# An attention and feed-forward kernel on one core: half of the score bounds computed by VectorE instead of GpSimd, weight loads spread over earlier stages, one activation table set for exponential and logarithm

## Chip, core and metric

One Trainium2 chip, one of its cores. The metric is the device time of one execution in microseconds (us). The profile shows one execution; its engines are named PE (TensorE matmul), PEld (TensorE weight load), DVE (VectorE), ACT (ScalarE), POOL (GpSimd) and SP (SyncE, which issues DMAs).

## What is computed

4096 tokens of 256 channels pass through two layers. The first layer adds a state-space recurrence and a mixture of 64 experts (6 per token); the second adds an attention and a gated feed-forward net. The change touches the second layer's attention. There, for each token, the 16 heads are the *positions* that attend to each other's channels: with Q, K and V reshaped to 16 x 64,

```
Q, K, V = ((x @ W + b).reshape(b, s, H, C) for each of the three)      # H, C = 16, 64; Q also times 1/8
scores = jnp.einsum('bshq,bshk->bshqk', Q, K)                          # an outer product of channels, per token and head
scores = jnp.where(triu(ones((C, C)), 1), -inf, scores)                # key channel k only up to query channel q
w = softmax(scores, axis=-1)
attn = jnp.einsum('bshqk,bshk->bshq', w, V).reshape(b, s, H * C)
y = attn @ Wo + bo + down(silu(gate(x)) * up(x))
```

So there is no matrix product in the attention itself: per token and head it is 64 x 64 / 2 products, exponentials and sums.

## The kernel before

The program is a sequence of stages with a barrier between them: routing; the recurrence; `routed_experts` (32 turns of 8 blocks); `combine` (adds the six expert outputs of each token, normalises, and stores x and its transpose); and `attention_and_ffn`, which takes three quarters of the time. In `combine` SP loads the expert outputs in a ring of five (L1065) and, after the first five, all weights of the last stage in one go (L1073 to L1080): bo, the three projections (1 MB each), three biases spread over the partitions, Wo, and three integer weights that VectorE turns into floats (L985 on).

`attention_and_ffn` works through 32 tiles of 128 tokens. A tile has 24 chunks: 0 to 7 are the triangle of the first half of the query channels, 8 to 15 the rectangle of second half queries on first half keys (2048 elements per partition each), 16 to 23 the triangle of the second half. The triangles' chunks have 2048, 256, 1536, 768, 1024, 1280, 512, 1792 and 2048, 1792, 1536, 1280, 1024, 256, 512, 768 elements. Every chunk goes through five steps on four engines:

- **product** (VectorE, `products`, L1215 and L1216, output `at_s`): query by key, the keys held in a PSUM bank `at_kp`;
- **subtraction** (GpSimd, L1280, in place on `at_s`): minus `at_m`, the greatest score that this query can have;
- **exponential** (ScalarE, L1365, in place);
- **value product** (VectorE, `times_v`, L1215 and L1216, output `at_pv`): times V, held in the PSUM bank `at_vp`;
- **row sums** (TensorE, L1525) of the exponentials into `at_den`, and of the value products into `at_num`.

The order on each engine is written out by hand in that engine's `tile(t, u)`, a loop over the chunk number c; VectorE makes the product of chunk c (one ahead in chunks 4 to 8) and then the value product of chunk c - 3. Beside the chunks each engine has small tasks at fixed c. TensorE projects the next tile's K at c = 4 and 8, its first query half at c = 17 and its first value half at c = 19, all into one shared PSUM bank `at_work`, so each projection waits until the one before has been read. ScalarE reads the query projection out in `keep_q` (c = 19 for the next tile's first half, c = 0 for the second half). At c = 18 it does the `silu` of the feed-forward net, which needs another table set than the exponential.

The bound `at_m` is needed by a tile's subtractions: max(q, 0) times the running maximum of the keys (`at_k_top`) minus max(-q, 0) times the running minimum (`at_k_low`). VectorE scans the keys (`scan`, c = 8 to 13). ScalarE writes max(q, 0) into `at_m` and max(-q, 0) into `at_fall` (L1318, L1320), and GpSimd does the rest in `maxima`, three operations of 512 elements (L1260, L1262, L1265), for the second half of this tile after chunks 3, 4, 5 and for the first half of the next tile after chunks 21, 22, 23. The first two read the scans `turned`, that is channels descending, with a step of 64 floats from one element to the next:

```
turned = lambda x: view(x[:], [[-1, RANGE], [C, H]], h * RANGE + RANGE - 1)
MAXIMA_HERE, MAXIMA_NEXT = {3: 0, 4: 1, 5: 2}, {21: 0, 22: 1, 23: 2}
```

Of the kernel before, what the change touches and what calls it, by code (L numbers as in the profile page):

```python
# [6 lines left out]
ALU = mybir.AluOpType  # L7
# [640 lines left out]
def routed_experts(nc, k, io, scratch):  # L648
# [3 lines left out]
    with ExitStack() as ctx:  # L652
# [36 lines left out]
        with nc.Block(no_gpsimd_drain=True) as block:  # L689
# [189 lines left out]
            def _(sp):  # L879
# [27 lines left out]

                for i in range(TURNS):
                    turn_in(i)


def combine(nc, k, io, scratch):
    with ExitStack() as ctx:
# [14 lines left out]
        x2_done, x2_out, bo_in, w_in, dequant = (a.sem(s) for s in ("x2", "x2_out", "bo_in", "w_in", "dequant"))  # L928
        y_in, xT_out = [a.sem(f"y_in{j}") for j in range(RING)], [a.sem(f"xT_out{j}") for j in range(TURN_RING)]
        dve_step, pool_step = a.sem("dve"), a.sem("pool")  # L930
        members = lambda g: slice(g * GROUP, (g + 1) * GROUP)
        with nc.Block(no_gpsimd_drain=True) as block:
# [11 lines left out]
            def _(dve):  # L944
# [10 lines left out]
                def weights(step):  # L955

                    if step == 0:
                        dve.wait_ge(w_in, 160)
# [15 lines left out]
                    elif step == 4:  # L974
                        c(v.tensor_copy(parts[96:128, :], rest[96:128, :]))
                    else:
                        dequantise(step - 5)
# [82 lines left out]
            def _(sp):  # L1060
# [13 lines left out]
                for i, name in enumerate(("WqT", "WkT", "WvT")):  # L1074
                    sp.dma_start(k.wqkv[i][:], io[name].rearrange("(c p) n -> p c n", p=P)).then_inc(w_in, 16)
                for i, name in enumerate(("bq", "bk", "bv")):
                    sp.dma_start(rest[:, i * HC:(i + 1) * HC], io[name].partition_broadcast(P)).then_inc(w_in, 16)
                sp.dma_start(k.wo[:], io["Wo"].rearrange("(c p) n -> p c n", p=P)).then_inc(w_in, 16)
                for i, (name, c) in enumerate((("wgT", DC), ("wuT", DC), ("wdT", HT))):
                    sp.dma_start(stage[i][:].rearrange("p (c n) -> p c n", c=c),  # L1080
                                 io[name].rearrange("(c p) n -> p c n", p=P)).then_inc(w_in, 16)
# [10 lines left out]
                sp.wait_ge(x2_out, 16 * NT // GROUP)  # L1092
                for j in range(TURN_RING):
# [22 lines left out]
FIRST, BODY = 2, 10  # L1116


def attention_and_ffn(nc, k, io, scratch):
    with ExitStack() as ctx:  # L1120
# [27 lines left out]
        work_done, k_out, q_out, v_out, up_out, scanned, max_step = (  # L1148
            a.sem(s) for s in ("work_done", "k_out", "q_out", "v_out", "up_out", "scanned", "max_step"))
# [68 lines left out]
        with nc.Block() as block:  # L1218
# [32 lines left out]
            def _(pool):  # L1251
                def maxima(t, h, step):

                    n = t * 2 + h
                    turned = lambda x: view(x[:], [[-1, RANGE], [C, H]], h * RANGE + RANGE - 1)
                    rows = lambda x, at=0: view(x[:], [[H, RANGE], [1, H]], at)
                    if step == 0:
                        pool.wait_ge(scanned, t * 4 + 4)
                        pool.wait_ge(q_out, n + 1)
# [3 lines left out]
                    else:  # L1263
                        pool.wait_ge(max_step, n * 3 + 2)
# [457 lines left out]
```

## Time and profile before

| | us |
|---|---|
| median of 3 runs (lowest to highest) | 3786.36 (3785.81 to 3789.21) |
| the profiled execution's own time | 3785.92 |
| its span, first to last instruction | 3784.2 |
| `combine`, about | 785 to 910 of the span |
| `attention_and_ffn`, about | 910 to 3784 of the span |
| one tile of it | 88.6 |
| busy in the whole span: PE, DVE, POOL, ACT | 3491.1, 3234.1, 3306.9, 1968.9 |
| mean granted clock of TensorE | 0.972 |

In the views, "idle before" is the time in which an engine did nothing before an instruction, with what ended it; a row of the timeline has the start, the length, the engine, the line, the operation, out<-in, and the count of merged instructions. Lengths of neighbours on one engine overlap by some hundredths of a us, so what an instruction takes of its engine is read from start to start. The granted clock is a share of TensorE's upper level.

### The profile page before, as it was taken

The page shows a single profiled execution, that of the slowest core. Times are in us where ns is not written, and L with a number is a line of the kernel's source. Part 1 is how long each engine was busy: PE and PEld are TensorE (multiplying, and loading weights), DVE is VectorE, ACT ScalarE, POOL GpSimd, SP SyncE. Part 2 cuts the span into 40 slices and gives each one's busy share as a digit, 9 for nine tenths or more (in the row PEclk, how much of TensorE's full clock was granted, in tenths as well). Part 3 has the DMA queues.
Part 4 walks back from the last instruction along what each step waited for, and adds up shares of the span by engine and source line. Part 5 has one row for each costly group of instructions (what it writes and reads, how often), then busy time and mean ns, then how long its engine had stood idle before and what let it go on. Part 6 is the DMA issues. An engine that isn't in the chain of part 4 may idle for free.

```text
span 3784.2 us, 72605 instructions
## 1 busy us (share of the span) xinstructions
PE 3491.1 (92%) x25868; PEld 3068.3 (81%) x26061; DVE 3234.1 (85%) x3516; ACT 1968.9 (52%) x2519; POOL 3306.9 (87%) x1507
## 2 busy tenths in 40 slices
PE   3684999967999999999999999999999999999999
PEld 2343988855888888888888888888888888888888
DVE  8422677757999999999999999999999999999998
ACT  1100434444555555665665566555555665665565
POOL 1677555523999999999999999999999999999998
PEclk7797999988999999999999999999999999999999
DMA  9523566685000000000000000000000000000000
GB/s 377 179 102 111 183 191 199 198 302 198 4 5 5 5 5 5 7 5 5 8 5 6 5 5 5 6 5 5 5 5 6 7 5 6 7 5 5 5 5 5
DMA packets 110619, 209.17 MB, mean 55 GB/s; under 512 B 16608, under 2 KB 77280, under 8 KB 110304
## 3 DMA queue, kind: packets, MB, share of 16 engines
q1 hardware_dynamic: 84192, 140.90, 11.4%
q0 software_dynamic: 21504, 59.93, 4.3%
q8 instruction: 191, 3.13, 0.3%
q10 hardware_dynamic: 4608, 4.20, 0.3%
q14 instruction: 124, 1.02, 0.1%
HBM read 183.34 MB, written 107.74 MB: 77 GB/s over the span
## 4 chain that ended last, share of the span: by engine, by line
POOL 43%; issue 31%; PE 1%; DVE 0%; ACT 0%; POOLq 0%; DMA 0%; ACTq 0%; DVEq 0%
POOL at_s L1280 38%; POOL at_m L1265 2%; POOL at_fall L1262 2%; POOL at_m L1260 2%; POOLq L1279 0%; DVE at_pv L1216 0%; PE at_work L1502 0%; PE at_num L1525 0%; ACT at_s L1365 0%; POOL at_hid L1270 0%; DVE at_s L1216 0%; DMA at_xT<-xT 0%; PE at_num L1502 0%; PE at_den L1525 0%; PE at_misc L1551 0%
## 5 line engine op out<-in xcount | busy, mean ns | idle before, releaser
L1280 POOL TENSOR_TENSOR at_s<-at_s,at_m 128x2048 f32<-128x2048 f32 (+7 forms) x768 | 2507.1, 3306 | 5.4 <-POOL at_m L1265 4.5
L1365 ACT ACTIVATE at_s<-at_s 128x2048 f32<-128x2048 f32 (+7 forms) x768 | 1081.7, 1417 | 952.6 <-POOL at_s L1280 952.2
L1525 PE MATMUL at_num<-k_ident,at_pv 128*128 128x128 f32 (+2 forms) x9216 | 1135.6, 273 | 65.5 <-DVE at_pv L1215 54.6
L1525 PE MATMUL at_den<-k_ident,at_s 128*128 128x128 f32 (+2 forms) x9216 | 1137.5, 273 | 19.7 <-ACT at_s L1365 17.2
L1525 PEld LDWEIGHTS at_num<-k_ident,at_pv 128*128 128x128 f32 (+2 forms) x9216 | 1025.3, 139 | 150.7 <-DVE at_pv L1215 84.3
L1525 PEld LDWEIGHTS at_den<-k_ident,at_s 128*128 128x128 f32 (+2 forms) x9216 | 1028.5, 139 | 57.8 <-ACT at_s L1365 21.2
L1216 DVE TENSOR_TENSOR at_pv<-at_s,at_vp 128x2048 f32<-128x2048 f32 (+7 forms) x512 | 690.6, 1349 | 122.1 <-PE at_num L1525 66.5
L1216 DVE TENSOR_TENSOR at_s<-at_q,at_kp 128x2048 f32<-128x2048 f32 (+7 forms) x512 | 689.9, 1348 | 27.4 <-PE at_den L1525 23.8
L1215 DVE TENSOR_TENSOR at_pv<-at_s,at_vp 128x2048 f32<-128x2048 f32 x256 | 583.9, 2281 | 0.0
L1215 DVE TENSOR_TENSOR at_s<-at_q,at_kp 128x2048 f32<-128x2048 f32 x256 | 581.4, 2271 | 0.0
L706 POOL DMA_INDIRECT picked<-moe_yo,moe_row x256 | 245.8, 960 | 171.0 <-ACT moe_yo L761 82.9
L1502 PE MATMUL at_work<-k_region,at_xT 128*128 128x512 f32 x776 | 367.0, 595 | 7.4 <-DMA at_xT<-xT 7.4
L142 POOL DMA_INDIRECT slot_x<-e_xn,e_slot x192 | 190.6, 993 | 136.9 <-DMA slot_x<-k_region 75.7
L728 PE MATMUL moe_gu<-moe_xT,c_w 128*128 128x128 f32 x2048 | 278.3, 279 | 5.6 <-DVE moe_xT L850 5.6
L728 PEld LDWEIGHTS moe_gu<-moe_xT,c_w 128*128 128x128 f32 x2048 | 250.3, 193 | 17.2 <-DVE moe_xT L850 13.1
L1502 PEld LDWEIGHTS at_work<-k_region,at_xT 128*128 128x128 f32 x776 | 132.9, 191 | 101.5 <-issue 93.6
L767 ACT ACTIVATE moe_gate<-moe_gu 128x128 f32<-128x128 f32 x256 | 71.0, 277 | 269.5 <-PE moe_gu L728 269.5
L1512 PE MATMUL at_work<-at_xT,k_region 128*128 128x128 f32 x1536 | 187.2, 275 | 0.0
L1512 PEld LDWEIGHTS at_work<-at_xT,k_region 128*128 128x128 f32 x1536 | 179.1, 192 | 0.0
L844 DVE TENSOR_TENSOR moe_hid<-moe_gate,moe_gu 128x128 f32<-128x128 f32 x256 | 73.4, 287 | 104.7 <-ACT moe_gate L767 101.3
L735 PE MATMUL moe_yp<-c_w,moe_hid 128*128 128x256 f32 x512 | 153.5, 382 | 0.3 <-DVE moe_hid L844 0.3
L850 DVE COPY moe_xT<-moe_tr 128x256 f32<-128x256 f32 x256 | 107.1, 418 | 46.5 <-PE moe_tr L719 45.1
(249 smaller groups left out, 3171.2 us busy)
## 6 DMA issues: line engine op xcount, KB each, us to landing
c_w<-experts SPq DMA_DIRECT2D x256, 384.0 KB
slot_x<-k_region SPq DMA_DIRECT2D x16, 2144.0 KB, 25.1
moe_x<-slot_x SPq DMA_DIRECT2D x256, 134.0 KB, 2.2
cmb_y<-picked SPq DMA_DIRECT2D x32, 768.0 KB, 7.8
at_xT<-xT SPq DMA_DIRECT2D x33, 128.0 KB, 2.0
e_x<-u SPq DMA_DIRECT2D x4, 1024.0 KB, 9.5
picked<-moe_yo,moe_row POOLq DMA_INDIRECT x256
xT<-cmb_xT ACTq DMA_DIRECT2D x32, 128.0 KB, 6.0
```

What stands on the lines that cost most here:

```text
L142: nc.gpsimd.indirect_dma_start(scratch["slot_x"], bass.IndirectOffsetOnAxis(ap=k.slot[:, n, j:j + 1], axis=0), k.xn[:, n, :], None).then_i ...
L706: pool.indirect_dma_start(scratch["picked"], bass.IndirectOffsetOnAxis(ap=row[i % 2][:, j:j + 1], axis=0), yo[j][:], None).then_inc(y_out[ ...
L728: ins = nc.tensor.matmul(gu[j % 2][:, s, :], w[j][:, (2 * s + c) * P:(2 * s + c + 1) * P], xT[j][:, c, :], start=(c == 0), stop=(c == DC - 1))
L735: nc.tensor.matmul(yp[j % 2][:], hid[j][:], w[j][:, 2 * D:3 * D], start=True, stop=True).then_inc(y_done, 1)
L850: nc.vector.tensor_copy(xT[j][:], tr[j % 2][:]).then_inc(xT_ready, 1)
L1215: return nc.vector.tensor_tensor(by_row(out), by_row(other), keys, ALU.mult)
L1216: return nc.vector.tensor_tensor(out, other, keys, ALU.mult)
L1280: nc.gpsimd.tensor_tensor(part(s_slot, c), part(s_slot, c), by_query(m[unit_of(c)][:], c), ALU.subtract).then_inc(sub_done, 1)
L1365: nc.scalar.activation(part(s_slot, c), part(s_slot, c), ACT.Exp, scale=C ** -0.5).then_inc(exp_done, 1)
L1502: nc.tensor.matmul(into[:], xT[u][:, c, :], wqkv[which][:, c, cols], start=(c == 0), stop=False)
L1512: ins = nc.tensor.matmul(work[:, (2 * s + h) * P:(2 * s + h + 1) * P], w[:, c, tile * P:(tile + 1) * P], xT[u][:, c, :], start=(c == 0), s ...
L1525: ins = nc.tensor.matmul(dst[0:wide, b * P:(b + 1) * P], buf[:, at:at + wide], k.ident[:], start=(c in (0, NTRI) and x == 0 and b == 0), s ...
```

## The change

**Maxima.** For the first query half, ScalarE now copies the projection only (`keep_q` returns after the copy), and VectorE makes the bound in three operations that read the projection's bank directly: `at_m` = `at_k_top` x q, the bank = `at_k_low` x q (in place), `at_m` = the greater of the two. The first two stand at VectorE's c = 20, the third at c = 21, of the tile before. GpSimd keeps the second half's maxima. TensorE's next projection into that bank (its c = 19) now waits for the third operation.

**Table sets.** A table set with both exponential and logarithm is loaded before the stage and after each `silu`.

**Loads.** The three projections are loaded in turns 10, 18 and 26 of `routed_experts`, biases, integer weights and Wo between the loads of `combine`'s ring. (One small tensor, gamma, moves to another place in a shared region.)

```diff
 # routed_experts, SyncE
+                def load_projection(which):
+                    tiles = (which + 1) * HC * DC // D
+                    sp.wait_ge(own_added, tiles)
+                    sp.dma_start(k.wqkv[which][:], io[("WqT", "WkT", "WvT")[which]].rearrange("(c p) n -> p c n", p=P)
+                                 ).then_inc(k.wqkv_in, 16)
+                PROJECTION = {10: 0, 18: 1, 26: 2}
                 for i in range(TURNS):
                     turn_in(i)
+                    if i in PROJECTION:
+                        load_projection(PROJECTION[i])
...
 # combine, SyncE
+                BIAS, STAGE, WO = {5: 0, 6: 1, 7: 2}, {9: 0, 11: 1, 13: 2}, 16
                 for n in range(RING, NT):
                     load(n)
+                    if n in BIAS:
+                        load_bias(BIAS[n])
+                    if n in STAGE:
+                        load_stage(STAGE[n])
+                    if n == WO:
+                        sp.dma_start(k.wo[:], io["Wo"].rearrange("(c p) n -> p c n", p=P)).then_inc(w_in, 16)
...
 # attention_and_ffn, GpSimd
-                MAXIMA_HERE, MAXIMA_NEXT = {3: 0, 4: 1, 5: 2}, {21: 0, 22: 1, 23: 2}
+                MAXIMA_HERE = {3: 0, 4: 1, 5: 2}
...
-                        if c in (0, NTRI):
-                            pool.wait_ge(max_step, t * 6 + (3 + 3 * unit_of(c)))
+                        if c == 0:
+                            pool.wait_ge(max0_step, t * 3 + 3)
+                        if c == NTRI:
+                            pool.wait_ge(max_step, t * 3 + 3)
...
-                        if c in MAXIMA_NEXT:
-                            maxima(t + 1, 0, MAXIMA_NEXT[c])
...
 # ScalarE, keep_q
+                    if h == 0:
+                        nc.scalar.copy(q[h][:, FRONT:QL], source[:]).then_inc(q_out, 1)
+                        return
...
 # ScalarE, end of silu
+                    nc.scalar.preload_act_table_set(EXP_AND_LN)
...
 # VectorE
+                def maxima(t, step, source=work):
+                    turned = lambda x: view(x[:], [[-1, RANGE], [C, H]], RANGE - 1)
+                    rows = lambda x, at=0: view(x[:], [[H, RANGE], [1, H]], at)
+                    if step == 0:
+                        dve.wait_ge(q_out, t * 2 + 1)
+                        dve.wait_ge(scanned, t * 4 + 4)
+                        wait(dve, sub_done, (t - 1) * NCH + NTRI)
+                        v.tensor_tensor(rows(m[0], FRONT), turned(k_top), rows(source), ALU.mult).then_inc(max0_step, 1)
+                    elif step == 1:
+                        dve.wait_ge(max0_step, t * 3 + 1)
+                        v.tensor_tensor(rows(source), turned(k_low), rows(source), ALU.mult).then_inc(max0_step, 1)
+                    else:
+                        dve.wait_ge(max0_step, t * 3 + 2)
+                        v.tensor_tensor(m[0][:, FRONT:QL], source[:], m[0][:, FRONT:QL], ALU.max).then_inc(max0_step, 1)
...
+                MAXIMA_NEXT = {20: (0, 1), 21: (2,)}
...
+                        for step in MAXIMA_NEXT.get(c, ()):
+                            maxima(t + 1, step)
...
 # TensorE, c = 19
                         pe.wait_ge(q_out, t * 2 + 3)
+                        pe.wait_ge(max0_step, t * 3 + 6)
                         project(t + 1, 1 - u, 2, 0)
```

VectorE in the second triangle of a tile, before, with what each waits for: the product of chunk 20, the value product of chunk 17, the first step of a division, the product of 21 and the value product of 18 (`at_exp` is the exponential's semaphore, `at_q_out` that of `keep_q`).

```order
L1216 TENSOR_TENSOR at_s<-at_q,at_kp 128x1024 [waits at_pv,at_den_done]
L1216 TENSOR_TENSOR at_pv<-at_s,at_vp 128x1792 [waits at_num_done,at_exp]
L1440 TENSOR_TENSOR at_den<-at_den,at_inv 128x512 [waits at_inv_ready]
L1216 TENSOR_TENSOR at_s<-at_q,at_kp 128x256 [waits at_pv,at_den_done]
L1216 TENSOR_TENSOR at_pv<-at_s,at_vp 128x1536 [waits at_num_done,at_exp]
L1443 SCALAR_TENSOR_TENSOR at_log_den<-at_den,at_inv 128x512 [waits at_newton]
```

The same place in the changed kernel:

```order
L1240 TENSOR_TENSOR at_s<-at_q,at_kp 128x1024 [waits at_pv,at_den_done]
L1240 TENSOR_TENSOR at_pv<-at_s,at_vp 128x1792 [waits at_num_done,at_exp]
L1471 TENSOR_TENSOR at_m<-at_k_top,at_work 128x512 [waits at_sub,at_scanned,at_q_out]
L1474 TENSOR_TENSOR at_work<-at_k_low,at_work 128x512 [waits at_max0_step]
L1484 TENSOR_TENSOR at_den<-at_den,at_inv 128x512 [waits at_inv_ready]
L1240 TENSOR_TENSOR at_s<-at_q,at_kp 128x256 [waits at_pv,at_den_done]
L1240 TENSOR_TENSOR at_pv<-at_s,at_vp 128x1536 [waits at_num_done,at_exp]
L1477 TENSOR_TENSOR at_m<-at_work,at_m 128x512 [waits at_max0_step]
L1487 SCALAR_TENSOR_TENSOR at_log_den<-at_den,at_inv 128x512 [waits at_newton]
```

Two operations came in behind the value product of chunk 17, the first with a wait for ScalarE's copy of the query, and one behind that of chunk 18.

ScalarE around its c = 18 and 19 in the changed kernel: the exponential of chunk 18 (1536 elements), `silu` between two table loads, the exponential of chunk 19 (1280), the copy of the next tile's query.

```order
L1391 ACTIVATE at_s<-at_s 128x1536
L1379 ACT_TABLE_LOAD
L1379 ACTIVATE at_hid<-at_gu_sb 128x768
L1380 ACT_TABLE_LOAD
L1391 ACTIVATE at_s<-at_s 128x1280
L1339 COPY at_q<-at_work 128x512
L1391 ACTIVATE at_s<-at_s 128x1024
```

Before, the same stood there with two more activations behind the copy (into `at_m` and `at_fall`); the four other table loads of a tile, two in front of each logarithm and exponential of the denominators, are gone elsewhere.

## Rows read from the trace of the kernel before

**Rows 1.** Page, part 1: busy us (share of the span) x instructions, whole span.

```profile
PE 3491.1 (92%) x25868; PEld 3068.3 (81%) x26061; DVE 3234.1 (85%) x3516; ACT 1968.9 (52%) x2519; POOL 3306.9 (87%) x1507
```

**Rows 2.** Busy us, sum and mean of twelve tiles' stretches; last numbers: mean per engine.

```profile
sum 1063.80, PE 1037.83 PEld 935.48 DVE 1011.63 ACT 636.13 POOL 1060.56; mean PE 86.49 PEld 77.96 DVE 84.30 ACT 53.01 POOL 88.38
```

**Rows 3.** Timeline of VectorE from chunk 20 to the next tile's start.

```profile
1625.28 2.02 DVE L1216 TENSOR_TENSOR at_pv<-at_s,at_vp 128x1792 f32<-128x1792 f32 x1
1627.21 0.69 DVE L1440 TENSOR_TENSOR at_den<-at_den,at_inv 128x512 f32<-128x512 f32 x1
1627.82 0.41 DVE L1216 TENSOR_TENSOR at_s<-at_q,at_kp 128x256 f32<-128x256 f32 x1
...
1629.81 0.69 DVE L1443 SCALAR_TENSOR_TENSOR at_log_den<-at_den,at_inv 128x512 f32<-128x512 f32 x1
...
1634.99 2.29 DVE L1216 TENSOR_TENSOR at_s<-at_q,at_kp 128x2048 f32<-128x2048 f32 x1
...
1642.64 1.22 DVE L1216 TENSOR_TENSOR at_s<-at_q,at_kp 128x1024 f32<-128x1024 f32 x1 [0.71 <-PE at_den L1525]
1647.18 2.29 DVE L1216 TENSOR_TENSOR at_pv<-at_s,at_vp 128x2048 f32<-128x2048 f32 x1 [3.31 <-PE at_num L1525]
```

**Rows 4.** Timeline of ScalarE around chunks 18 and 19 and the next tile's start.

```profile
1623.11 1.49 ACT L1365 ACTIVATE at_s<-at_s 128x1536 f32<-128x1536 f32 x1 [0.73 <-POOL at_s L1280]
1624.62 1.28 ACT L1354 ACT_TABLE_LOAD   x1
1625.91 0.84 ACT L1354 ACTIVATE at_hid<-at_gu_sb 128x768 f32<-128x768 f32 x1
1626.77 1.28 ACT L1365 ACT_TABLE_LOAD   x1
1628.07 1.28 ACT L1365 ACTIVATE at_s<-at_s 128x1280 f32<-128x1280 f32 x1
1629.24 0.57 ACT L1316 COPY at_q<-at_work 128x512 f32<-128x512 f32 x1
...
1646.48 0.61 ACT L1340 COPY at_vp<-at_v 128x512 f32<-128x512 f32 x1
```

**Rows 5.** Timeline of GpSimd, end of one tile and of the next.

```profile
1549.73 4.55 POOL L1280 TENSOR_TENSOR at_s<-at_s,at_m 128x2048 f32<-128x2048 f32 x1 [0.16 <-POOL at_m L1265]
...
1630.87 1.56 POOL L1260 TENSOR_TENSOR at_m<-at_k_top,at_m 128x512 f32<-128x512 f32 x1
...
1633.62 1.53 POOL L1262 TENSOR_TENSOR at_fall<-at_k_low,at_fall 128x512 f32<-128x512 f32 x1
...
1636.89 1.28 POOL L1265 TENSOR_TENSOR at_m<-at_m,at_fall 128x512 f32<-128x512 f32 x1
1638.34 4.56 POOL L1280 TENSOR_TENSOR at_s<-at_s,at_m 128x2048 f32<-128x2048 f32 x1 [0.17 <-POOL at_m L1265]
```

**Rows 6.** Timeline of VectorE: one instruction that waits for another; first idle time of `combine`.

```profile
793.71 0.42 DVE L1003 TENSOR_TENSOR e_x<-e_x,cmb_acc 128x256 f32<-128x256 f32 x1 [1.57 <-PE cmb_acc L1025]
794.17 0.43 DVE L1005 BATCH_NORM_STATS2 cmb_stats<-e_x 128x6 f32<-128x256 f32 x1
...
821.88 0.48 DVE L983 SCALAR_TENSOR_TENSOR e_x<-cmb_y,e_choice_w,e_x 128x256 f32<-128x256 f32 x1 [20.39 <-DMA cmb_y<-picked]
```

**Rows 7.** Groups of VectorE instructions, 780 to 785 us: busy us, mean ns.

```profile
L873 DVE TENSOR_REDUCE moe_weight_sum<-e_choice_w 128x32 f32<-128x192 f32 x1 | 0.5, 482 | 0.0
L876 DVE TENSOR_TENSOR e_choice_w<-e_choice_w,moe_weight_sum 128x192 f32<-128x192 f32 x1 | 0.4, 358 | 0.0
```

**Rows 8.** Timeline of TensorE at its c = 19: the next tile's value projection.

```profile
1633.54 1.88 PE L1502 MATMUL at_work<-k_region,at_xT 128*128 128x512 f32 x4
```

**Rows 9.** Busy us per stretch (length, engines, PEclk, DMA share, GB/s): experts' end, `combine`.

```profile
700.00:770.00 70.00, 69.05 (x521) 62.72 (x520) 49.28 (x173) 28.02 (x87) 41.40 (x43) 1.00 0.70 215
790.00:822.00 32.00, 12.34 (x51) 10.32 (x51) 5.78 (x18) 9.31 (x31) 1.27 (x2) 0.71 1.03 382
822.00:907.00 85.00, 72.89 (x334) 59.95 (x334) 71.88 (x167) 47.91 (x147) 13.82 (x14) 0.94 0.91 327
```

More of the change, by code:

```diff
@@ L976, in weights @@
                     else:
+                        dve.wait_ge(stage_in, 48)
                         dequantise(step - 5)
@@ L1073, in _, with load_bias, load_stage @@
                 sp.dma_start(bo[:], io["bo"].partition_broadcast(P)).then_inc(bo_in, 16)
[L1074 to L1079, printed above, removed]
+                def load_bias(i):
+                    sp.dma_start(rest[:, i * HC:(i + 1) * HC], io[("bq", "bk", "bv")[i]].partition_broadcast(P)
+                                 ).then_inc(bias_in, 16)
+                def load_stage(i):
+                    name, c = (("wgT", DC), ("wuT", DC), ("wdT", HT))[i]
                     sp.dma_start(stage[i][:].rearrange("p (c n) -> p c n", c=c),
-                                 io[name].rearrange("(c p) n -> p c n", p=P)).then_inc(w_in, 16)
+                                 io[name].rearrange("(c p) n -> p c n", p=P)).then_inc(stage_in, 16)
+                BIAS, STAGE, WO = {5: 0, 6: 1, 7: 2}, {9: 0, 11: 1, 13: 2}, 16
                 for n in range(RING, NT):
                     load(n)
+                    if n in BIAS:
[4 more added lines that the diff above has]
+                        sp.dma_start(k.wo[:], io["Wo"].rearrange("(c p) n -> p c n", p=P)).then_inc(w_in, 16)
                     if n % GROUP == 0 and n >= 3 * GROUP:
@@ L1092, in _ @@
                 sp.wait_ge(x2_out, 16 * NT // GROUP)
+                sp.wait_ge(w_in, 16)
+                sp.wait_ge(k.wqkv_in, 48)
                 for j in range(TURN_RING):
@@ L1116 @@
 FIRST, BODY = 2, 10
+EXP_AND_LN = "natural_log_exp_and_others"
 def attention_and_ffn(nc, k, io, scratch):
@@ L1147, in attention_and_ffn @@
         xT_in = [a.sem(f"xT_in{u}") for u in range(2)]
-        work_done, k_out, q_out, v_out, up_out, scanned, max_step = (
-            a.sem(s) for s in ("work_done", "k_out", "q_out", "v_out", "up_out", "scanned", "max_step"))
+        work_done, k_out, q_out, v_out, up_out, scanned, max_step, max0_step = (
+            a.sem(s) for s in ("work_done", "k_out", "q_out", "v_out", "up_out", "scanned", "max_step",
+                              "max0_step"))
         kp_ready, vp_ready, mult_done, sub_done, exp_done, pv_done = (
@@ L1251, in _, with maxima @@
             def _(pool):
-                def maxima(t, h, step):
-                    n = t * 2 + h
+                def maxima(t, step):
+                    h = 1
                     turned = lambda x: view(x[:], [[-1, RANGE], [C, H]], h * RANGE + RANGE - 1)
@@ L1282, in tile @@
                         if c in MAXIMA_HERE:
-                            maxima(t, 1, MAXIMA_HERE[c])
-                        if c in MAXIMA_NEXT:
-                            maxima(t + 1, 0, MAXIMA_NEXT[c])
+                            maxima(t, MAXIMA_HERE[c])
                         if c == GATED:
@@ L1293, in _ @@
                     nc.gpsimd.memset(t[:, FULL:FULL + TAIL], 0.0).then_inc(zeroed, 1)
-                for step in range(3):
-                    maxima(0, 0, step)
                 pool.wait_ge(padded, 4)
@@ L1318, in keep_q @@
                     nc.scalar.activation(m[h][:, FRONT:QL], source[:], ACT.Relu)
-                    wait(act, max_step, n * 3)
+                    wait(act, max_step, t * 3)
                     nc.scalar.activation(fall[:], source[:], ACT.Relu, scale=-1.0).then_inc(q_out, 1)
@@ L1391, in tile @@
                             show_k(t + 1, 1 - u, 0)
+                nc.scalar.preload_act_table_set(EXP_AND_LN)
                 keep_k(0, 0, 0)
@@ L1427, in scan @@
                         dve.wait_ge(work_done, use)
-                        wait(dve, max_step, t * 6)
+                        wait(dve, max_step, t * 3)
+                        wait(dve, max0_step, t * 3)
                         v.tensor_tensor_scan(k_top[:, cols], flat(keep_max), source[:], 0.0, ALU.add, ALU.max
@@ L1486, in _ @@
                         scan(0, half, step, half + 1, source=(work, first_k)[half])
+                for step in range(3):
+                    maxima(0, step, source=first_q)
                 dve.wait_ge(padded, 4)
@@ L1614, in _ @@
                 pe.wait_ge(q_out, 1)
+                pe.wait_ge(max0_step, 3)
                 pe.wait_ge(v_out, 1)
@@ L1643, in carve @@
         return parts
-    k.xnT, k.bT, k.cT, k.sgT, k.suT, k.sdT, k.gamma, k.beta, k.zeros, k.bu = carve(first)
+    k.xnT, k.bT, k.cT, k.sgT, k.suT, k.sdT, k.beta, k.zeros, k.bu, k.gamma = carve(first)
     k.xs, k.xnT = k.xnT, k.xnT.rearrange("p n (c t) -> p n c t", c=DC)
```

10 lines of the change are left out of this document (6 added, 4 removed).

## The prediction

> **What bounds the kernel now.** I read the page's busy shares first: TensorE, GpSimd and VectorE are at 85% or more and ScalarE is at half [rows 1], so the shares alone name no bound. The stretches tile by tile, second, do: in a tile of 88.65 us (1063.80 / 12) GpSimd works 88.4, TensorE 86.5, VectorE 84.3 [rows 2]. GpSimd has no slack. VectorE's 4.3 us of idle time are not spread: the timeline shows 0.71 and 3.31 us just ahead of and at the tile's first value product [rows 3]. The label there is TensorE, but what ended the wait is ScalarE's copy into `at_vp`, over at 1646.48 + 0.61 = 1647.09, and VectorE starts at 1647.18 [rows 3, 4]. That copy stands behind the exponential of chunk 0, hence behind GpSimd's subtraction of chunk 0, hence behind VectorE's product of chunk 0. So this idle time follows VectorE's own product; it is not a reserve that can be spent anywhere. A tile's length is 1638.34 - 1549.73 = 88.61 us, from one subtraction of chunk 0 to the next [rows 5].
>
> **The maxima, what is removed.** GpSimd loses three operations a tile, all between the subtractions of chunk 21 and the next chunk 0: 1.56, 1.53 and 1.28 us, 4.4 in all [rows 5]. ScalarE loses two activations behind its copy. If GpSimd alone decided, a tile would fall to 84.2.
>
> **What is added, and where it waits.** The first new VectorE operation needs ScalarE's copy of the query. Before, that copy ends at 1629.24 + 0.57 = 1629.81 [rows 4], and VectorE reaches the place, behind the value product of chunk 17, at 1627.21 [rows 3]. So VectorE would stand 2.60 us in front of it. The copy can't come earlier: it stands behind the exponential of chunk 19, this behind table load, `silu`, table load, and these behind the exponential of chunk 18, which follows GpSimd's subtraction of chunk 18 (ScalarE waited 0.73 us for it) [rows 4]. Behind the waiting instruction on VectorE are all products of chunks 21, 22, 23 and of the next tile's chunk 0, so GpSimd, which gained 4.4 us just there, gets nothing to work on.
>
> This closes a loop, and its length is the new tile. Step by step: (a) from a subtraction of chunk 0 to the copy's end, 1629.81 - 1549.73 = 80.08 us: in it GpSimd runs without a pause up to chunk 18 and ScalarE from there, and nothing of it is removed. (b) From the copy to VectorE's start 0.09, as after `at_vp` above. (c) First maximum. A 512-element operation on a PSUM bank lasts 0.69 and takes 0.61 of the engine [rows 3]. Its successor waits for it, which costs the full length and 0.04 (794.17 against 793.71 + 0.42 [rows 6]): 0.73. For its reading with a step between elements I add 0.33: the strided reduction of 192 elements takes 482 ns, a plain operation of 192 takes 358 [rows 7], 0.65 ns an element, times 512. So 1.06. (d) Second maximum: 0.61 + 0.33 = 0.94. (e) What VectorE does today from the division to the end of the next tile's product of chunk 0: 1634.99 + 2.29 - 1627.21 = 10.07 [rows 3]; in its midst the third maximum, 0.61. (f) To the subtraction's start 0.17, as today [rows 5]. The sum is 80.08 + 0.09 + 1.06 + 0.94 + 10.07 + 0.61 + 0.17 = 93.02 us, 4.41 more than 88.61. There are 31 passages from one tile to the next: 31 x 4.41 = 136.7 us.
>
> The one price in it that the trace doesn't show directly is the strided reading. Its lower end is nothing (0.66 us a tile, 20 us in all, less); the upper is the value taken, which is the nearest row. The Trainium skill, in VectorE: DVE Perf Modes, Mode 1x (REGULAR), says of the baseline mode that "weird strides" work and a result comes each cycle; by that the penalty would be nothing and the sum 20 us lower. The strided row speaks against it, but it is another operation, and no row here shows the very one.
>
> **TensorE's new wait.** Its c = 19 projection starts at 1633.54 [rows 8]. In the changed order the third maximum ends at 1629.81 + 0.09 + 1.06 + 0.94 + 2.60 + 0.69 = 1635.19 (2.60 for the division, product 21 and value product 18, 1629.81 - 1627.21 [rows 3]): TensorE is held 1.65 us, with row sums queued behind. It has 88.6 - 86.5 = 2.1 us idle a tile and gets 4.4 more, so I take 0 for it; if it weren't made up, 31 x 1.65 = 51 us.
>
> **Table sets.** Four loads of 1.28 us [rows 4] a tile leave ScalarE. It is busy 53 of 88.6 us [rows 2], and none of the four lies in the loop above (the two around `silu` stay). Cost and gain 0.
>
> **Loads.** Today VectorE waits 20.39 us in `combine` for the sixth expert output [rows 6], behind the weights, while DMA is full (1.03); afterwards DMA is still 0.91 busy and VectorE 71.9 of 85 us [rows 9]. So only what leaves the stage is won: three projections, 3.1 MB, at 382 to 327 GB/s [rows 9] 8 to 9.6 us; I take 9. The ends are 0 (if VectorE's and TensorE's own work fills the time) and the whole 20.4. In the experts' stage DMA has 0.30 of 70 us free [rows 9], 21 us, and a projection needs about 3 us; TensorE is the bound there with 69.05 of 70. SP issues each one behind a turn's loads, and the states it waits for are added two turns earlier. I take 1 us for all three, between 0 and 10. The first tile's maxima change one for the other: 0. The last tile's delay the drain, where TensorE is last: 1, between 0 and 4.4.
>
> **Sum.** 3785.92 (the profiled execution's own time) + 136.7 - 9 + 1 + 1 = 3915.6. The median of the runs is 0.4 above that execution: **3916 us**, 3.4% slower. With the ends of the terms this case spans 3881 (no stride penalty, 20 us from the loads) to 3938.
>
> **Rivals.** *A, faster:* VectorE doesn't wait, because its idle 4.0 us move from the tile's start to the copy and the moved work lands in slack. Then VectorE is the bound: 84.3 + 2.6 = 86.9 us a tile, just above TensorE's 86.5: 31 x -1.7 = -53, and with the loads 3786 - 53 - 9 + 2 = 3726. It decides by one thing, whether the copy ends before VectorE is through with chunk 17's value product; for it speaks that GpSimd is the busiest engine, against it the 2.60 us above, and that the idle time at the tile's start comes behind the product of chunk 0 in any case. The Trainium skill (Perfetto Trace Analysis, Identifying the Most-Contended Engine) would have the engine with the highest occupancy, here GpSimd, relieved first, and by it this rival would be the forecast. The trace bears the occupancy out but shows a loop that leaves GpSimd's relieved place aside. *B, no change:* the added wait and the idle time at the tile's start cancel, a tile stays at 88.6 and only the loads count: 3786 - 9 + 2 = 3779. It would need a shorter chain from chunk 0's product to `at_vp`, of which the change removes nothing. *C, slower still:* TensorE can't make up its 1.65 us: 3916 + 51 = 3967. For it, 86.5 busy of 88.6; against it, the longer tile. That the table loads or the loads stay where they were is excluded by the order of the instructions.
>
> **How the numbers follow.** The forecast 0.80, A 0.10, B 0.05, C 0.05. A change of 0.2%, 7.6 us, is about what a measurement of this kernel can tell from none; B lies on that edge, so I give 0.03 of it to no change and 0.02 to faster. Faster 0.12, same 0.03, slower 0.85. The range takes in the forecast's own 3881 to 3938 and a part of what lies beyond it on both sides (TensorE not making up all): 3870 to 3945.
>
> **What would show it.** Right: a tile of about 93 us; on VectorE a wait of some 2.6 us in front of the first maximum, ended by ScalarE; GpSimd busy about 84 us a tile and idle ahead of chunks 21 to 0, waiting for VectorE's products; the first two maxima about 1.0 us long, the third 0.7; two table loads a tile; `combine` shorter by some 9 us with no idle time of 20. Wrong: a tile under 88.6 us, or the first maximum starting with no wait. That the maxima last 0.7 us throughout would take 20 us off and leave the rest standing.

## The result, and the profile after

| us | before | after |
|---|---|---|
| median (lowest to highest) | 3787.36 (3785.81 to 3789.21), 4 runs | 3911.37 (3909.72 to 3912.42), 4 runs |
| profiled span | 3784.2 | 3910.6 |
| first load of the attention issued | 910.60 | 898.20 |
| from there to the end | 2873.6 | 3012.4 |
| one tile | 88.61 | 93.04 |

After / before is 1.0327 (95%: 1.0315 to 1.034): slower by 124 us, within the range given, 5 us below the forecast. The attention is 138.8 us longer and begins 12.4 us earlier.

The page of the changed kernel, busy us in the whole span, answers to [rows 1]. GpSimd works 138 us less, ScalarE 193 less, VectorE 87 more, and the program is longer.

```profile
PE 3528.3 (90%) x25868; PEld 3085.2 (79%) x26061; DVE 3320.8 (85%) x3615; ACT 1776.0 (45%) x2325; POOL 3168.4 (81%) x1408
```

Two tiles of it (length, then busy us and instructions of PE, PEld, DVE, ACT, POOL; PEclk, DMA share, GB/s), against [rows 2]: GpSimd is down from 88.4 to 84.1 us, VectorE up from 84.3 to 86.9, and the tile is longer than either.

```profile
1661.89:1754.95 93.06, 88.53 (x690) 79.49 (x696) 86.87 (x63) 46.99 (x48) 84.16 (x29) 1.00 0.02 5
1754.95:1847.97 93.02, 87.02 (x679) 77.92 (x683) 86.89 (x63) 47.01 (x48) 84.13 (x28) 1.00 0.02 5
```

VectorE's timeline at the place of the change. Between the same value product and the division, where [rows 3] has no wait, it now stands 2.72 us in front of the first maximum, for ScalarE's copy `at_q`. The 3.3 us at the tile's start are still there (3.13).

```profile
1742.16 1.06 DVE L1471 TENSOR_TENSOR at_m<-at_k_top,at_work 128x512 f32<-128x512 f32 x1 [2.72 <-ACT at_q L1339]
1743.25 1.05 DVE L1474 TENSOR_TENSOR at_work<-at_k_low,at_work 128x512 f32<-128x512 f32 x1
...
1746.80 0.68 DVE L1477 TENSOR_TENSOR at_m<-at_work,at_m 128x512 f32<-128x512 f32 x1
...
1752.59 2.28 DVE L1240 TENSOR_TENSOR at_s<-at_q,at_kp 128x2048 f32<-128x2048 f32 x1
...
1763.78 2.29 DVE L1240 TENSOR_TENSOR at_pv<-at_s,at_vp 128x2048 f32<-128x2048 f32 x1 [3.13 <-ACT at_s L1391]
```

ScalarE there: the exponential of chunk 19 and behind it the copy, in the order of [rows 4].

```profile
1740.21 1.27 ACT L1391 ACTIVATE at_s<-at_s 128x1280 f32<-128x1280 f32 x1
1741.39 0.57 ACT L1339 COPY at_q<-at_work 128x512 f32<-128x512 f32 x1
```

GpSimd at the end of the tile: in [rows 5] it worked through here; now it stands before chunks 21, 22, 23 and 0, 8.9 us together, each time for VectorE's product. What it lost in maxima (4.4 us) it got back twice over as waiting.

```profile
1745.30 0.73 POOL L1306 TENSOR_TENSOR at_s<-at_s,at_m 128x256 f32<-128x256 f32 x1 [3.09 <-DVE at_s L1240]
1748.76 1.28 POOL L1306 TENSOR_TENSOR at_s<-at_s,at_m 128x512 f32<-128x512 f32 x1 [2.73 <-DVE at_s L1240]
1751.62 1.83 POOL L1306 TENSOR_TENSOR at_s<-at_s,at_m 128x768 f32<-128x768 f32 x1 [1.58 <-DVE at_s L1240]
1754.95 10.46 POOL L1306 TENSOR_TENSOR at_s<-at_s,at_m 128x2048 f32<-128x2048 f32 x4 [1.50 <-DVE at_s L1240]
```

TensorE's projection, the one that stands in [rows 8]: held 1.68 us behind the third maximum.

```profile
1747.54 1.98 PE L1551 MATMUL at_work<-k_region,at_xT 128*128 128x512 f32 x4 [1.68 <-DVE at_m L1477]
```

These rows give one round of the loop step by step. From the subtraction of chunk 0 (1661.89) to the copy's end (1741.39 + 0.57 = 1741.96) it is 80.07 us; to the first maximum 0.20; from there to the end of the next product of chunk 0 (1752.59 + 2.28 = 1754.87) 12.71; to the subtraction (1754.95) 0.08. Together that is 93.06.

The three new operations in 30 tiles (busy us, mean ns; idle time before, with what ended it): the two that read in steps last 1066 and 1053 ns, the third, over as many elements, 683.

```profile
L1471 DVE TENSOR_TENSOR at_m<-at_k_top,at_work 128x512 f32<-128x512 f32 x30 | 32.0, 1066 | 82.5 <-ACT at_q L1339 82.5
...
L1474 DVE TENSOR_TENSOR at_work<-at_k_low,at_work 128x512 f32<-128x512 f32 x30 | 31.6, 1053 | 1.0
...
L1477 DVE TENSOR_TENSOR at_m<-at_work,at_m 128x512 f32<-128x512 f32 x31 | 21.2, 683 | 0.0
```

### The profile page after: what moved, and what is told of

Its sections match the earlier page's. It is cut to its first block, busy times and chain, and to the rows that moved or that the text cites. A ratio compares the mean times of both kernels' runs of the same rounds, so it can differ in the third digit from the quotient of the medians.

```text
span 3910.6 us, 72503 instructions
## 1 busy us (share of the span) xinstructions
PE 3528.3 (90%) x25868; PEld 3085.2 (79%) x26061; DVE 3320.8 (85%) x3615; ACT 1776.0 (45%) x2325; POOL 3168.4 (81%) x1408
## 3 DMA queue, kind: packets, MB, share of 16 engines
q8 instruction: 191, 3.13, 0.3%
## 4 chain that ended last, share of the span: by engine, by line
POOL 39%; issue 34%; PE 0%; DVE 0%; ACT 0%; POOLq 0%; DVEq 0%; ACTq 0%
POOL at_s L1306 34%; POOL at_hid L1294 1%; POOL at_fall L1286 1%; POOL at_m L1284 1%; POOL at_m L1289 1%; POOLq L1305 0%; PE at_num L1574 0%; DVE at_s L1240 0%; PE at_work L1551 0%; PE at_den L1574 0%; PE at_misc L1600 0%; ACT L1379 0%; ACT L1380 0%; DVE at_m L1471 0%; PE at_misc L1606 0%
## 5 line engine op out<-in xcount | busy, mean ns | idle before, releaser
L1551 PE MATMUL at_work<-k_region,at_xT 128*128 128x512 f32 x776 | 375.0, 606 | 63.3 <-DVE at_m L1477 51.6
```

Source lines behind the costliest of these rows:

```text
L1551: nc.tensor.matmul(into[:], xT[u][:, c, :], wqkv[which][:, c, cols], start=(c == 0), stop=False)
```

## The experiments

The theory under test is the prediction's: a tile is the loop GpSimd (to the subtraction of chunk 18), ScalarE (to the copy), VectorE (maxima, to the product of the next chunk 0), GpSimd. Rival A says that busy time sets the tile, rival C that TensorE does. "A tile" below is read from one subtraction of chunk 0 to another; ratios are to the kernel before, intervals are 95%.

### One part alone: the loads

The change's first two hunks (loads in `routed_experts` and between the ring's loads in `combine`) in the kernel before; all else as before.

> The kernel before with the change's loads alone (GpSimd keeps all maxima, the table sets stay). Theory (all of the loss is in the attention's tiles, the loads are a gain of their own): attention begins some 12 us earlier, as in the trace after (898.2 against 910.6), a tile stays at 88.6 us, total 3787 - 12 = about 3775. Rival (the loads cost time, for instance the experts' stage is longer by more than combine is shorter, and the tiles lose less than 4.4 us): 3790 or more.

3771.44 us (3767.93 to 3773.72), 0.9959 (0.9945 to 0.9973): 16.0 less, where 12 were expected. A tile is untouched:

```profile
1531.80 10.47 POOL L1302 TENSOR_TENSOR at_s<-at_s,at_m 128x2048 f32<-128x2048 f32 x4 [0.17 <-POOL at_m L1287]
...
1620.40 5.25 POOL L1302 TENSOR_TENSOR at_s<-at_s,at_m 128x2048 f32<-128x2048 f32 x2 [0.17 <-POOL at_m L1287]
```

So the loads are a gain of their own, and what the change lost it lost elsewhere. Where the gain is from shows in SP's queue. Before, the weights' issue (start, length) holds up the ring, one of them for 10.44 us, and the ring goes on only at 808.55:

```profile
796.34 10.44 SPq L1080 DMA_DIRECT2D cmb_stage<-wgT  x1
...
808.55 24.93 SPq L1065 DMA_DIRECT2D cmb_y<-picked  x8
```

In the changed kernel VectorE waits 7.53 and 2.75 us for the first two expert outputs (7.49 and 1.42 before). Behind these its longest wait is 2.56 us, where one was 20.39 [rows 6]:

```profile
820.03 0.48 DVE L995 SCALAR_TENSOR_TENSOR e_x<-cmb_y,e_choice_w,e_x 128x256 f32<-128x256 f32 x1 [2.56 <-DMA cmb_y<-picked]
```

From `combine`'s first load to the attention's first load it takes 125.1 us before, 109.6 with the change and 108.0 with the loads alone: 15.5 and 17.1 us less. The whole stretch, before and in the changed kernel (the last figure is GB/s):

```profile
785.50:910.60 125.10, 85.46 (x384) 70.49 (x384) 77.91 (x184) 61.80 (x192) 15.11 (x17) 0.86 0.93 336
```

```profile
788.63:898.20 109.57, 86.58 (x384) 70.87 (x384) 78.20 (x184) 61.85 (x193) 15.47 (x17) 0.89 0.94 355
```

125.10 us at 336 GB/s are 42.0 MB, 109.57 at 355 are 38.9. The 3.1 MB of the three projections are gone, worth 9.3 us at the old rate, and the remaining bytes move at a higher rate, worth 6.2 us more. The stretch that answers to the second of [rows 9] shows TensorE and VectorE working beside the transfers, 27.44 and 16.70 us of 32 against 12.34 and 5.78. Whether this overlap or the new order of the loads raised the rate, no run separates.

```profile
790.00:822.00 32.00, 27.44 (x115) 22.98 (x116) 16.70 (x46) 19.84 (x64) 2.83 (x4) 0.88 0.99 389
```

### One part alone: the table sets

```diff
 # after each silu, and once before the stage
+                    nc.scalar.preload_act_table_set(EXP_AND_LN)
```

> The kernel before with the change's table sets alone. Theory (the four loads of 1.28 us a tile that go lie on no path that sets the end): 3787, within 4 us. Rival (ScalarE's delay is felt by GpSimd or VectorE): each load that lies on the path gives back 1.28 us a tile, 31 x 1.28 = 40 us, so 3747 or 3707.

3785.55 us (3783.93 to 3788.87), 0.9997 (0.9988 to 1.0007); a tile 88.60. Four loads of 1.28 us a tile are gone and nothing came of it, as forecast.

### The maxima one chunk later

```diff
-                MAXIMA_NEXT = {20: (0, 1), 21: (2,)}
+                MAXIMA_NEXT = {21: (0, 1), 22: (2,)}
```

> The changed kernel with the three maxima one chunk later in VectorE's order (c = 21 and 22). Theory (a tile is the loop from the subtraction of chunk 0 over ScalarE's copy to the next product of chunk 0): the 2.60 us of the division, product 21 and value product 18 leave the piece behind the copy and fill the wait, so a tile is 93.02 - 2.60 = 90.4 us and the total 3911 - 31 x 2.6 = about 3830; GpSimd still idle ahead of chunks 22 to 0. Rival A (VectorE's or GpSimd's busy time sets the tile): the same work in another order, 3911. Rival C (TensorE, held behind the third maximum): it is held as long as before or longer, 3911 or more.

3830.85 us (3827.55 to 3835.35), 1.0112 (1.0096 to 1.0129): 80.5 less than the changed kernel, 2.60 a tile. VectorE goes from the value product of chunk 18 to the first maximum with no wait on the row; the work is the same, on the same engines. ScalarE's copy ends at 1722.15, VectorE's value product at 1722.22: the move has used up the wait, and the two now arrive together.

```profile
1721.58 0.57 ACT L1339 COPY at_q<-at_work 128x512 f32<-128x512 f32 x1
```

```profile
1720.47 1.75 DVE L1240 TENSOR_TENSOR at_pv<-at_s,at_vp 128x1536 f32<-128x1536 f32 x1
1722.35 1.08 DVE L1471 TENSOR_TENSOR at_m<-at_k_top,at_work 128x512 f32<-128x512 f32 x1
```

Rival A in its simple form, that busy time sets the tile of the changed kernel, falls.

### The copy first

```diff
 # ScalarE, at the head of the loop over c (and gone behind the exponential)
+                        if c == KEEP_Q0:
+                            keep_q(t + 1, 0, work_use(t, "Q0"))
                         act.wait_ge(sub_done, count(t, c))
```

> The changed kernel with one instruction moved: ScalarE's copy of the next tile's query ahead of the exponential of chunk 19 instead of behind it. Theory (the loop runs through that copy): it ends 1.2 us earlier, the wait in front of the first maximum falls from 2.7 to 1.5 us, a tile is 91.8 us, total 3911 - 31 x 1.2 = about 3874. Rival A (busy time sets the tile): nothing is taken from any engine, 3911. Rival C (TensorE): its sums of chunk 19 come 0.5 us later, 3911 or more.

3875.96 us (3872.42 to 3876.99), 1.0231 (1.0214 to 1.0249): 35.4 less, 1.14 a tile. ScalarE, now with the copy right behind the table load:

```profile
1546.00 1.28 ACT L1380 ACT_TABLE_LOAD   x1
1547.29 0.59 ACT L1339 COPY at_q<-at_work 128x512 f32<-128x512 f32 x1
```

VectorE's wait for it in the same tile is 1.54 us, as expected:

```profile
1548.08 1.10 DVE L1471 TENSOR_TENSOR at_m<-at_k_top,at_work 128x512 f32<-128x512 f32 x1 [1.54 <-ACT at_q L1339]
```

### The first maximum twice

```diff
+                        v.tensor_tensor(rows(m[0], FRONT), turned(k_top), rows(source), ALU.mult).then_inc(again, 1)
+                        dve.wait_ge(again, t + 1)
                         v.tensor_tensor(rows(m[0], FRONT), turned(k_top), rows(source), ALU.mult).then_inc(max0_step, 1)
```

> The changed kernel with the first maximum computed twice, the second time behind a wait for the first. Theory (everything between the copy and the product of chunk 0 is in the loop): a tile is longer by the operation's full 1.06 us and 0.03, 94.1 us, total 3911 + 31 x 1.09 = about 3945. Rival A (VectorE has 93.0 - 86.8 us of room a tile): 3911.

3944.35 us (3942.97 to 3950.33), 1.0419 (1.0402 to 1.0437): 33.0 more, 1.06 a tile. VectorE, with the wait for the copy unchanged and 1.10 from one first maximum to the other:

```profile
1744.73 1.07 DVE L1472 TENSOR_TENSOR at_m<-at_k_top,at_work 128x512 f32<-128x512 f32 x1 [2.71 <-ACT at_q L1340]
1745.83 1.05 DVE L1474 TENSOR_TENSOR at_m<-at_k_top,at_work 128x512 f32<-128x512 f32 x1
```

### The division first

```diff
 # VectorE, c = 20 and 21
-                        for step in MAXIMA_NEXT.get(c, ()):
-                            maxima(t + 1, step)
...
                             divide(t, 0, DIVIDE_HERE[c])
+                        for step in MAXIMA_NEXT.get(c, ()):
+                            maxima(t + 1, step)
```

> The changed kernel with VectorE's step of the division at c = 20 ahead of the first two maxima instead of behind them (at c = 21 likewise). Theory: the 0.61 us of that step pass from behind the copy into the wait ahead of it, a tile is 92.4 us, total 3911 - 31 x 0.61 = about 3892. Rival A (busy time sets the tile): no work is removed, 3911.

3892.08 us (3890.54 to 3894.12), 1.0276 (1.0259 to 1.0293): 19.3 less, 0.62 a tile. No instruction was added or taken; one passed from behind the copy to the front of it, into the wait:

```profile
1733.73 0.69 DVE L1484 TENSOR_TENSOR at_den<-at_den,at_inv 128x512 f32<-128x512 f32 x1
1736.51 1.07 DVE L1471 TENSOR_TENSOR at_m<-at_k_top,at_work 128x512 f32<-128x512 f32 x1 [2.08 <-ACT at_q L1339]
```

### The third maximum later

```diff
-                MAXIMA_NEXT = {20: (0, 1), 21: (2,)}
+                MAXIMA_NEXT = {20: (0, 1), 22: (2,)}
```

> The changed kernel with the third maximum alone one chunk later (c = 22 instead of 21). Theory (the loop contains the third maximum at either place, and TensorE makes up what it is held): TensorE is held some 4 us instead of 1.7 ahead of its projection, the tile stays at 93.0 us, 3911 within 8 us. Rival C (TensorE's hold is paid): 31 x 2.5 = 78 us more, about 3990, or a part of it.

3943.33 us (3941.98 to 3946.7), 1.0413 (1.0396 to 1.0431): 32.0 more, 1.03 a tile. The theory said none, rival C 78. TensorE's projection and what follows it:

```profile
1752.17 3.78 PE L1551 MATMUL at_work<-k_region,at_xT 128*128 128x512 f32 x4 [3.50 <-DVE at_m L1477]
1756.17 2.54 PE L1574 MATMUL at_num<-k_ident,at_pv 128*128 128x128 f32 x12 [0.22 <-issue]
```

The hold grew from 1.68 to 3.50 us, and behind it TensorE ran slowly: the projection lasts 3.78 us instead of 1.98, the next row sums 2.54 instead of 1.47 (in the changed kernel). The stretch's eighth figure is the granted clock, 0.63 here and 1.00 in the same place of the changed kernel, so part of it ran at the lower level, 1.2 GHz:

```profile
1750.00:1756.00 6.00, 3.78 (x4) 1.55 (x6) 6.00 (x7) 1.15 (x2) 3.08 (x2) 0.63 0.01 3
```

So 1.82 us more of hold cost TensorE 1.82 + 1.80 + 1.07 = 4.7 us, more than it makes up by the next tile's start, where VectorE waits for its sums:

```profile
1758.82 0.69 DVE L1240 TENSOR_TENSOR at_pv<-at_s,at_vp 128x512 f32<-128x512 f32 x1 [1.25 <-PE at_num L1574]
...
1764.41 1.22 DVE L1240 TENSOR_TENSOR at_s<-at_q,at_kp 128x1024 f32<-128x1024 f32 x1 [1.22 <-PE at_den L1574]
```

The delay reaches the loop on GpSimd. In the middle of the tile, where it has no pause in the changed kernel, it now stands 0.50, 0.78 and 0.15 us for VectorE's products of the rectangle:

```profile
1811.22 4.57 POOL L1306 TENSOR_TENSOR at_s<-at_s,at_m 128x2048 f32<-128x2048 f32 x1 [0.78 <-DVE at_s L1239]
```

"TensorE makes it up" therefore holds for the change's 1.68 us and not for any hold.

### Values shown early

```diff
 # ScalarE, at the head of the loop over c (and gone behind chunk 1's exponential)
+                        if c == 0:
+                            show_v(t, 0)
                         act.wait_ge(sub_done, count(t, c))
```

> The changed kernel with ScalarE's first copy of the values (into the bank that the value products read) ahead of the exponential of chunk 0 instead of behind that of chunk 1. Theory (that idle time of VectorE lies beside the loop): VectorE's 3.1 us at a tile's start fall below 1 us, its wait in front of the first maximum grows by as much, the tile stays at 93.0 us, 3911 within 8 us. Rival A (VectorE's busy and idle time together set the tile, so that any idle time taken away is won): 31 x 2.3 = 71 us less, about 3840.

3914.47 us (3908.53 to 3915.6), 1.033 (1.0313 to 1.0348): no change, as the theory says. But the time did not go where it said. The wait at the tile's start fell from 3.13 to 0.48; the wait for the copy stayed at 2.71; the rest is in new, small waits, for the exponential (1.40) and for TensorE (1.23):

```profile
1734.90 2.29 DVE L1240 TENSOR_TENSOR at_pv<-at_s,at_vp 128x2048 f32<-128x2048 f32 x1 [1.40 <-ACT at_s L1393]
...
1742.96 1.08 DVE L1473 TENSOR_TENSOR at_m<-at_k_top,at_work 128x512 f32<-128x512 f32 x1 [2.71 <-ACT at_q L1339]
...
1762.31 2.29 DVE L1240 TENSOR_TENSOR at_pv<-at_s,at_vp 128x2048 f32<-128x2048 f32 x1 [0.48 <-ACT at_s L1393]
...
1767.76 0.69 DVE L1240 TENSOR_TENSOR at_s<-at_q,at_kp 128x512 f32<-128x512 f32 x1 [1.23 <-PE at_den L1576]
```

TensorE, too, waits longer at its projection, and is slow behind it, at a granted clock of 0.54. Here GpSimd has no pause in the middle of the tile, and no time is lost by it.

```profile
1748.37 3.78 PE L1553 MATMUL at_work<-k_region,at_xT 128*128 128x512 f32 x4 [2.78 <-DVE at_m L1479]
```

```profile
1749.00:1755.00 6.00, 5.78 (x19) 3.68 (x19) 6.00 (x6) 2.31 (x4) 3.11 (x2) 0.54 0.01 3
```

### Three moves together, and a fourth

Maxima one chunk later, copy first and values shown early, in one kernel.

> The changed kernel with three moves together: maxima one chunk later, copy of the query ahead of chunk 19's exponential, first copy of the values ahead of chunk 0's exponential. Theory: the loop through the copy is 93.0 - 2.6 - 1.2 = 89.2 us a tile, VectorE's own work 86.8 and about 1 of idle time, so the loop decides: total 3911 - 31 x 3.8 = about 3793. Rival C (TensorE, held behind the third maximum for some 2 us and more and then at its lower clock, cannot follow): 3830 or more. Rival A (each of the three moves adds its whole gain, 80, 35 and 71 us): about 3725.

3828.88 us (3824.54 to 3829.7), 1.0111 (1.0094 to 1.0128), no better than the maxima one chunk later by itself. The forecast of 3793 failed, and so did the sum of three gains. The figure is rival C's (3830 or more), its reason is not: over a tile TensorE works 86.80 of 90.32 us at a granted clock of 1.00, and its hold is 1.70 us, as in the changed kernel.

```profile
1636.46:1726.78 90.32, 86.80 (x679) 78.02 (x683) 86.97 (x63) 47.18 (x48) 84.19 (x28) 1.00 0.02 6
```

The wait for the copy was gone with the first move, so the copy's move had nothing left to shorten, and what showing the values early frees comes back as waits for other engines. One such wait, 0.55 us, stands in front of the value product behind ScalarE's second copy of the values; a fourth move puts that copy ahead of its exponential too.

```diff
+                        if c == 17:
+                            show_v(t, 1)
                         act.wait_ge(sub_done, count(t, c))
```

> The kernel e8_three with the same fourth move. Theory: its tile of some 90.3 us is set by VectorE, which has no pause from the value product behind that copy (0.55 us of waiting there) to the next product of chunk 0; so the copy closes a second loop beside the one through the query's copy, the 0.55 us are won, and the total is 3829 - 31 x 0.55 = about 3812. Rival (TensorE, held 1.7 us behind the third maximum, sets the tile): 3829.

3807.7 us (3803.36 to 3808.44), 1.0048 (1.0032 to 1.0063): 21 less, as the theory says (about 3812) and against the rival's none. Of its tile VectorE works 86.94 us, and three waits are left, for the exponential, for row sums and (`remote`) for the projection of the keys: 86.94 + 0.82 + 1.01 + 0.94 = 89.71 of 89.75. Work and waits of any engine add up to the tile, so this sum by itself does not make VectorE the bound. For it speaks that GpSimd stands 1.86, 2.18 and 1.50 us in front of chunks 22, 23 and 0, each time for VectorE's product. But VectorE in turn waits for TensorE and ScalarE, and no run separates these. Its 86.9 us of work are the floor of any order of this work, and this kernel is 2.8 us above it.

```profile
1549.47 2.29 DVE L1240 TENSOR_TENSOR at_pv<-at_s,at_vp 128x2048 f32<-128x2048 f32 x1 [0.82 <-ACT at_s L1397]
...
1554.49 0.69 DVE L1240 TENSOR_TENSOR at_s<-at_q,at_kp 128x512 f32<-128x512 f32 x1 [1.01 <-PE at_den L1578]
...
1567.11 1.22 DVE L1461 TENSOR_TENSOR_SCAN at_k_top<-k_region,at_work 128x512 f32<-128x512 f32 x1 [0.94 <-remote]
```

### A version faster than both

Here VectorE gets only the third maximum, which waits for no copy of ScalarE's; loads and table sets as changed, values shown early.

```diff
 # the kernel before; GpSimd
-                MAXIMA_HERE, MAXIMA_NEXT = {3: 0, 4: 1, 5: 2}, {21: 0, 22: 1, 23: 2}
+                MAXIMA_HERE, MAXIMA_NEXT = {3: 0, 4: 1, 5: 2}, {21: 0, 22: 1}
 # VectorE, behind products(t, 0)
+                        if c == 0:
+                            dve.wait_ge(max_step, t * 5 + 2)
+                            v.tensor_tensor(m[0][:, FRONT:QL], m[0][:, FRONT:QL], fall[:], ALU.subtract
+                                            ).then_inc(max0_step, 1)
```

> The kernel before with the change's loads and table sets, the first two maxima left on GpSimd, the third alone on VectorE (behind the product of chunk 0, so that it waits for nothing), and ScalarE's first copy of the values ahead of the exponential of chunk 0. Theory (a tile's length is the longest of the busy engines and of the loops): no wait for ScalarE's copy enters VectorE's order, GpSimd loses 1.28 us of its 88.4 a tile, VectorE gets 0.61 on top of 84.3, a tile is about 87.3 us, total 3771 - 31 x 1.3 = about 3732, below both kernels. Rival (VectorE is the later one at a tile's start, since the subtraction of chunk 0 now waits for two of its operations): a tile of 88.6 or more, 3771 or more.

3758.7 us (3757.38 to 3761.3), 0.9926 (0.9909 to 0.9943): faster than both kernels, and 27 us slower than expected (the rival said 3771 or more). GpSimd works 87.11 us of a tile of 88.32 and stands 1.11 in front of chunk 0 for VectorE's third maximum. That is the rival's mechanism, and it took most of the gain of a tile.

```profile
1530.44:1618.76 88.32, 86.40 (x678) 77.97 (x683) 84.95 (x61) 47.90 (x50) 87.11 (x30) 1.00 0.02 5
```

```profile
1618.76 4.56 POOL L1305 TENSOR_TENSOR at_s<-at_s,at_m 128x2048 f32<-128x2048 f32 x1 [1.11 <-DVE at_m L1504]
```

VectorE had lost 1.45 us earlier in the tile, in front of the value product behind the second copy of the values. The last kernel moves that copy as in the fourth move above.

```profile
1602.67 2.29 DVE L1239 TENSOR_TENSOR at_pv<-at_s,at_vp 128x2048 f32<-128x2048 f32 x1 [1.45 <-ACT at_s L1396]
```

> The kernel b1_third_on_vector with ScalarE's second copy of the values a tile also ahead of its chunk's exponential (chunk 17). Theory from its trace: VectorE stands 1.45 us a tile in front of the first value product that reads that copy, and GpSimd stands 1.10 us in front of the subtraction of chunk 0 for VectorE; the first wait is the cause of the second, so with the copy earlier both go, a tile is 88.3 - 1.1 = 87.2 us, total 3759 - 31 x 1.1 = about 3725. Rival (TensorE, 86.5 busy of 88.3, or GpSimd's own 87.1 is the limit at once, or the exponential of chunk 17, now behind the copy, is late): 3740 to 3759.

3759.26 us (3757.84 to 3762.27), 0.9924 (0.9911 to 0.9938): the same; the expected 34 us did not come. That wait is gone, and those at the start of the tile, for TensorE's row sums, an exponential and the key projection (`remote`), have grown from 0.91 + 0.16 + 0.88 = 1.95 us to 0.53 + 0.30 + 0.30 + 1.23 + 0.88 = 3.24:

```profile
1625.21 1.22 DVE L1239 TENSOR_TENSOR at_s<-at_q,at_kp 128x1024 f32<-128x1024 f32 x1 [0.53 <-PE at_den L1563]
...
1626.73 2.29 DVE L1239 TENSOR_TENSOR at_pv<-at_s,at_vp 128x2048 f32<-128x2048 f32 x1 [0.30 <-ACT at_s L1398]
...
1629.32 1.49 DVE L1239 TENSOR_TENSOR at_s<-at_q,at_kp 128x1280 f32<-128x1280 f32 x1 [0.30 <-PE at_den L1563]
...
1632.37 0.69 DVE L1239 TENSOR_TENSOR at_s<-at_q,at_kp 128x512 f32<-128x512 f32 x1 [1.23 <-PE at_den L1563]
...
1644.91 1.22 DVE L1463 TENSOR_TENSOR_SCAN at_k_top<-k_region,at_work 128x512 f32<-128x512 f32 x1 [0.88 <-remote]
```

GpSimd still stands 0.88 us in front of chunk 0 for VectorE's third maximum, so the one wait was not the cause of the other by itself. What holds the two engines together there stays open. Most of this version's gain, 16 of 28 us, is that of the loads alone; its tile is 88.32 against 88.62 there, 31 x 0.30 = 9 us.

## Why the prediction was right

- **The loop.** Forecast 93.02 us a tile, found 93.02 and 93.06. That it comes so close is in part luck: the step from the copy to VectorE was 0.20 and not 0.09, the last step 0.08 and not 0.17, and the two cancel. The wait in front of the first maximum: forecast 2.60, found 2.72. That it is a loop and not a coincidence of sizes is shown by four runs that each change one term: the piece behind the copy shorter by 2.60, by 0.61, longer by 1.09, the copy earlier by 1.2 were to give -81, -19, +34 and -37 us, and gave -80.5, -19.3, +33.0 and -35.4.
- **The strided reading.** Forecast 0.33 us on each of two operations, found 0.38 and 0.37 (1066 and 1053 less 683 ns). The forecast's row was that of another operation and was a good guide. The Trainium skill (VectorE: DVE Perf Modes, Mode 1x (REGULAR)) says that odd strides work in that mode and shows one result a cycle; read as no penalty, as the prediction's lower end reads it, this case doesn't agree. The first and the third operation read one operand from PSUM and one from SBUF alike and both write SBUF. They differ in the step, in the order of the operands and in the arithmetic (product, maximum), and no run separated these.
- **TensorE.** Held 1.68 us against the 1.65 forecast, and made up. The reason given, room in the longer tile, was too general: 3.50 us were not made up, with a stretch at a lower granted clock behind them.
- **Loads.** The one mis-sized term: 9 us forecast, 15.5 found in the changed kernel. The bound of 20.4 held. The bytes moved out were sized rightly (9.3 us); what failed was "only what leaves the stage is won", since the bytes that stayed moved at 355 GB/s instead of 336, 6.2 us more.
- **Experts' stage.** 1 us forecast; `combine` began 3.1 us later in the changed kernel's trace, but not at all in that of the loads alone (785.46 against 785.50), so the 3.1 is not shown to be the change's.
- **Table sets and last tile.** No effect of the table sets, as said. 31 x 4.43 = 137.3 of the attention's 138.8 us are in the tiles, which leaves 1.5 for the first and the last, forecast 1.
- **Rivals.** A fell with the 2.60 us of the third experiment; its price sets VectorE's busy time as a tile, 86.9 us, and after four moves a tile was still 89.75. B fell too: the wait at the tile's start stayed, at 3.13 us. C fell for this kernel, where 1.68 us were made up, and in part came true with the third maximum later. The Trainium skill (Perfetto Trace Analysis, Identifying the Most-Contended Engine) would have the engine with the highest occupancy relieved first. Here that was GpSimd, relieved of 4.4 us, and the tile grew by as much.

From span to span the forecast was 136.7 - 9 + 1 + 1 = 129.7 us more, and 126.4 were found: -6.5 by the loads, +2.1 by the experts' stage, +0.6 by the tiles (31 x 0.02), +0.5 by the first and the last tile. The tenths are those of one trace on each side.

## What to carry to other kernels

A busy share tells what an engine does, not what waits for it: before work is moved to an engine with idle time, look up what ended that idle time, and place the moved work against the time at which its inputs are ready. A wait put into an in-order queue delays everything behind it; follow it round until it comes back to where it began. Where the sum of that round is longer than what any one engine works (here 93.0 us against 88.5 at most), it is the new period. Once one wait is taken away, expect the next one close behind it (0.07 us with the maxima one chunk later), and don't add up gains.

## What was not expected

TensorE's clock answered to holds of a few microseconds. Behind 1.68 us of idle time (the changed kernel) the projection lasted 1.98 us; behind 2.78 us (values shown early) and 3.50 us (the third maximum later) it lasted 3.78, in stretches with a granted clock of 0.54 and 0.63. The length of the hold alone doesn't give the price: behind 2.78 us in the kernel with the first maximum twice it lasted 2.94, in a stretch at 0.72, and the tile grew by no more than the added operation. A wait on TensorE can thus cost more than its own length; how much of that reaches the end depends on the room behind it, nothing in the one kernel and 1.03 us a tile in the other.
